# A graph-attention kernel whose first stage no longer writes normalised rows

## The chip, the cores and the metric

The kernel runs on one core of a Trainium2 chip. The metric is device time in microseconds (us), the median of several executions; less is better. The core has TensorE (PE, matrix products), VectorE (DVE), ScalarE (ACT), GpSimd (POOL), SyncE (SP, which here only issues transfers) and 16 DMA engines. PE reads its stationary operand in a separate instruction, LDWEIGHTS, which the profile lists as PEld.

## The reference, cut to what matters

```
x: [10000, 768] f32;  src, dst: 10000 edges sorted by dst, plus one self loop for each node
y  = (x - mean(x)) / sqrt(var(x) + 1e-5)                    # per row
h  = (y @ W1).reshape(N, 4, 512)
e  = leaky_relu(as_n[src] + ad_n[dst], 0.2)                 # as_n = sum_d h * a1_src, ad_n = sum_d h * a1_dst
alpha = softmax of e over the edges that share a dst
h1 = elu(segment_sum(alpha * h[src], dst) + b1)             # [N, 2048]
h2 = a second layer of the same kind with one head, 768 wide
x  = x + h2;   x = x + ffn(layernorm(x))
```

Because as_n = y @ (W1 a1_src), the kernel computes the eight logits of a node as the product of its row with eight vectors v1 [768, 8]. And because y[src] can be summed with its attention weights before the product with W1, layer 1 gathers rows of y, not of h.

## The kernel before

**Stages, one after the other, with a barrier between them.** `stage_normalise` makes normalised rows and logits; `stage_softmax` (sm1) gathers the logits of all edges and writes one record per edge (`rec1`); `stage_layers` does both layers' big products; `stage_softmax` (sm2), `stage_extra_rows` and `stage_output` finish.

**stage_normalise** takes 20 steps of 500 rows (NS = 20), each step four tiles of 125 rows (NT = 4), with four buffers (NB = 4). Before the first step DVE reduces W1 against a1_src and a1_dst to v1 (L349, 48 reductions). In a step DVE normalises in place (L321), takes the statistics of the next step (L289, L293, L295), and with POOL makes the f16 low parts (L327, L271); ACT makes the f16 high parts (L364) and copies transposed tiles out of PSUM (L374); PE transposes a tile (L390), multiplies with v1 as the stationary operand and 125 rows as the moving one (L398), and once a step turns the 8 x 500 logits back (L407), which costs DVE two copies (L316, L310). POOL does one power (L266). SP writes the two parts (`parts`, 1536 f16 values in a row, L238), loads the rows of the step four ahead (L226) and writes the logits (L231).

**stage_layers** works on 20 strips of 500 nodes; a strip is ten windows of 50 nodes (WPS = 10). For a window POOL gathers 128 rows of `parts` (78 edges and 50 own rows) by an indirect DMA into `rows`, which has two buffers (L1117); the gather of window i is issued when PE is done with window i-2. PE multiplies them with the attention weights, `ah` and `al` (L1358 to L1360, 18 products a window). ACT and DVE split the sums into f16 parts `zh` (L1311) and `zl` (L1201). A strip on PE is a first phase of 16 chunks of z @ W1 (L1394 to L1396) and a second phase of 64 steps of g @ W2 (L1418, L1419). The second phase of strip s also holds the windows of strip s+1: window n comes at step 1 + 6n (`AT_STEP`), so window products run between steps of the big product. For strip 0 the ten windows run alone ahead of everything, called the prologue below.

**Slots.** In each strip SP loads the records of the next strip's ten windows (L993, ten transfers) into `slots`, then starts a copy of x (L1076). At chunk 4 DVE computes the row indices from them (`slot_math`, L1165 to L1171); at chunks 5 to 9 it makes two masks each (L1176), which PE uses one chunk later in `look_up` (L1351); at chunk 12 come the weights, at 13 and 14 the first two `spread`. In the second phase DVE does, at window n, `low_parts(n)` (L1201) and `spread(n + 2)` (L1192 to L1196), ACT does `high_parts(n)` (L1311). Each tile of 125 nodes of the result goes through `h2` (L1278, L1280), which has two buffers.

Of the kernel before, what the change touches and what calls it, by code (L numbers as in the profile page):

```python
# [24 lines left out]
ALU = mybir.AluOpType  # L25
# [8 lines left out]
D = 768  # L34
# [17 lines left out]
REC = 12  # L52
# [113 lines left out]
POOL_LOWS = (1, 3)  # L166

def stage_normalise(nc, c, io, dr):

    with ExitStack() as ctx:
        m = Mem(nc, ctx, "nrm")
# [3 lines left out]
        v1 = m.sb("v1", [128, DC, 2 * HEADS])  # L177
        xb = m.sb("xb", [TN, NB, NT, D])
        parts = m.sb("parts", [TN, NB, NT, 2, D], F16)
        stats = m.sb("stats", [TN, NT, 2, 6])  # L180
        mv = m.sb("mv", [TN, NB, NT, 2])
# [3 lines left out]
        logit = m.sb("logit", [TN, NB, NT, 2 * HEADS])  # L185
        pt = [m.ps(f"pt{i}", [128, 2, 512]) for i in range(2)]
        pl = [m.ps(f"pl{i}", [2 * HEADS, NT, 128]) for i in range(2)]
        pb = [m.ps(f"pb{i}", [TN, NT, 2 * HEADS]) for i in range(2)]
        turned_logits = m.sb("turned_logits", [2 * HEADS, 2, NT, 128])
        weights, v_chain, init, held = m.sem("weights"), m.sem("v_chain"), m.sem("init"), m.sem("held")  # L190
        xin, stored, logits_out = ([m.sem(f"{n}{b}") for b in range(NB)] for n in ("xin", "stored", "logits_out"))
        held_pe, w1_in = m.sem("held_pe"), [m.sem(f"w1_in{k}") for k in range(DC)]
        chain, var_ready, pow_ready = m.sem("chain"), m.sem("var_ready"), m.sem("pow_ready")
        xs_ready, hi_ready, lo_ready, pool_lo_ready = (m.sem(n) for n in ("xs_ready", "hi_ready", "lo_ready", "pool_lo_ready"))
        turned, xt_ready, logits_done, row_ready, turned_back, logit_ready = (m.sem(n) for n in (
            "turned", "xt_ready", "logits_done", "row_ready", "turned_back", "logit_ready"))
        block = ctx.enter_context(nc.Block())
        x_rows = io["x"].rearrange("(s p t) d -> s p t d", p=TN, t=NT)
        t_rows = dr.parts.rearrange("(s p t) d -> s p (t d)", p=TN, t=NT)
        l_rows = dr.logit1.rearrange("(s p t) d -> s p (t d)", p=TN, t=NT)  # L200
        VECTOR_LOWS = [t for t in range(NT) if t not in POOL_LOWS]
# [16 lines left out]
        def _(sp):  # L218
# [5 lines left out]
            def load(s, b):  # L224
                for lo, hi in row_parts(TN):
                    sp.dma_start(xb[lo:hi, b], x_rows[s, lo:hi]).then_inc(xin[b], 16)  # L226

            def store_logits(s, b):
                hold(logit_ready, s + 1)
                for lo, hi in row_parts(TN):  # L230
                    sp.dma_start(l_rows[s, lo:hi], logit[lo:hi, b].rearrange("p t k -> p (t k)")).then_inc(logits_out[b], 16)  # L231

            def step(s, b, j):
                hold(hi_ready, NT * s + NT)
                hold(lo_ready, len(VECTOR_LOWS) * (s + 1))
                hold(pool_lo_ready, len(POOL_LOWS) * (s + 1))
                for lo, hi in row_parts(TN):
                    sp.dma_start(t_rows[s, lo:hi], parts[lo:hi, b].rearrange("p t k d -> p (t k d)")).then_inc(stored[b], 16)  # L238
                if within(s + NB):
                    hold(turned, NT * s + NT)  # L240
                    load(s + NB, b)
                if within(s - 2):
                    store_logits(s - 2, (b - 2) % NB)

            load(0, 0)
# [4 lines left out]
            for b in range(1, NB):  # L250
                load(b, b)
            rounds(sp, step)
            store_logits(NS - 2, NB - 2)
            store_logits(NS - 1, NB - 1)
            for b in range(NB):
                sp.wait_ge(stored[b], 32 * NJ)
                sp.wait_ge(logits_out[b], 32 * NJ)

        @block.gpsimd
        def _(pool):  # L260
# [3 lines left out]
            def rough_rstd(u, b):  # L264
                pool.wait_ge(var_ready, u + 1)
                nc.gpsimd.tensor_tensor(rough[:, b], ve[:, b], power[:], ALU.pow).then_inc(pow_ready, 1)  # L266

            def step(s, b, j):
                for t in POOL_LOWS:
                    pool.wait_ge(hi_ready, NT * s + t + 1)  # L270
                    nc.gpsimd.tensor_tensor(parts[:, b, t, 1], xb[:, b, t], parts[:, b, t, 0], ALU.subtract)\  # L271
                        .then_inc(pool_lo_ready, 1)
                if within(s + 1):
                    rough_rstd(s + 1, (b + 1) % NB)
# [5 lines left out]
        def _(dve):  # L280
            PER = 2 * NT + NT + 4

            def statistics(u, b, j):
# [3 lines left out]
                for t in range(NT):  # L287
                    for half in range(2):
                        q.put(nc.vector.bn_stats(stats[:, t, half], xb[:, b, t, half * (D // 2):(half + 1) * (D // 2)]))  # L289
# [7 lines left out]
            def refine(u, b):  # L297
# [6 lines left out]
                q.link(nc.vector.tensor_tensor(rstd[:, b], rough[:, b], sq[:], ALU.mult))  # L304

            def copy_logits(s, b, j):
                dve.wait_ge(turned_back, s + 1)
                if within(s, NB):
                    dve.wait_ge(logits_out[b], 32 * j)
                nc.vector.tensor_copy(logit[:, b], pb[b % 2][:]).then_inc(logit_ready, 1)  # L310

            def copy_rows(s, b):
                dve.wait_ge(logits_done, NT * s + NT)
                if within(s, 2):
                    dve.wait_ge(turned_back, s - 1)
                nc.vector.tensor_scalar(turned_logits[:, b % 2, :, 0:TN], pl[b % 2][:, :, 0:TN], 1.0 / SX, None, ALU.mult)\  # L316
                    .then_inc(row_ready, 1)

            def step(s, b, j):
                for t in range(NT):  # L320
                    nc.vector.tensor_scalar(xb[:, b, t], xb[:, b, t], mv[:, b, t, 0:1], rstd[:, b, t:t + 1], ALU.subtract,  # L321
                                            ALU.mult).then_inc(xs_ready, 1)
                if within(s + 1):
                    statistics(s + 1, (b + 1) % NB, j + (b + 1) // NB)
                for t in VECTOR_LOWS:
                    dve.wait_ge(hi_ready, NT * s + t + 1)
                    nc.vector.tensor_tensor(parts[:, b, t, 1], xb[:, b, t], parts[:, b, t, 0], ALU.subtract).then_inc(lo_ready, 1)  # L327
                if within(s - 1):
                    copy_rows(s - 1, (b - 1) % NB)
                if within(s + 1):  # L330
                    refine(s + 1, (b + 1) % NB)
                if within(s - 2):
                    copy_logits(s - 2, (b - 2) % NB, j - (b < 2))

            nc.vector.memset(xt[:], 0.0).then_inc(init, 1)
            statistics(0, 0, 0)
            refine(0, 0)

            ch = Chain(dve, v_chain)
            dve.wait_ge(weights, 32)  # L340
            for k in range(DC):
                dve.wait_ge(w1_in[k], 16)
                for side, a in ((0, asrc), (1, adst)):
                    for h in range(HEADS):
                        cols = slice(h * HID, h * HID + HID)
                        at = side * HEADS + h
                        if ch.n >= 2:
# [3 lines left out]
                            op0=ALU.mult, op1=ALU.add, accum_out=v1[:, k, at:at + 1]))  # L351
            rounds(dve, step)
            copy_rows(NS - 1, NB - 1)
            copy_logits(NS - 2, NB - 2, NJ - 1)
            copy_logits(NS - 1, NB - 1, NJ - 1)

        @block.scalar
        def _(act):
            def step(s, b, j):
                for t in range(NT):  # L360
                    act.wait_ge(xs_ready, NT * s + t + 1)
                    if t == 0 and within(s, NB):
                        act.wait_ge(stored[b], 32 * j)
# [1641 lines left out]
```

## Time and profile before

| | |
|---|---|
| median of 3 runs | 4167.94 us (4165.6 to 4171.07) |
| profiled execution | 4167.93 us, span 4166.2 us |
| busy | PE 3571.3 us (86%), DVE 2228.8 (53%), ACT 1354.7 (33%), POOL 850.1 (20%) |
| first stage | 0 to about 293 us |
| sm1 | about 293 to 583 us |
| layers | about 583 to 3482 us |
| sm2, extra rows, output | to the end |

The profile gives, for each engine, busy time and the idle time ahead of an instruction with what ended it. PE's granted clock is in tenths or as a share of full speed (1.00 is 2.4 GHz, 0.50 is 1.2 GHz). The profiled execution's span lies 1.7 us below its time, and its time is the median of the runs.

### The profile page before, as it was taken

What the parts mean: (1) busy time and instruction counts of PE and PEld (TensorE: products, weight loads), DVE (VectorE), ACT (ScalarE), POOL (GpSimd) and SP (SyncE); (2) the same over time, 40 slices, a digit from 0 to 9 for tenths busy, and PEclk for the clock granted to TensorE, in tenths of its full rate; (3) what the DMA queues carried; (4) which work ended last, traced back from release to release, by engine and by line L of the source; (5) the groups of instructions that cost most, each with busy time, mean ns of one, the idle gap of its engine ahead of it and who ended that gap; (6) DMA issues with size and microseconds to landing.
All of it is one profiled execution on the core that took longest, in us unless ns stands there. A gap on an engine that the chain in (4) does not pass through costs nothing. (4 is left out here: it accounts for less than half of the span.)

```text
span 4166.2 us, 68773 instructions
## 1 busy us (share of the span) xinstructions
PE 3571.3 (86%) x22440; PEld 2183.9 (52%) x22441; DVE 2228.8 (53%) x5433; ACT 1354.7 (33%) x2327; POOL 850.1 (20%) x1236
## 2 busy tenths in 40 slices
PE   4860019999999999999999999999999996388888
PEld 3640015565556556655655565566556654256565
DVE  8877345334434443443344344434443434699998
ACT  2531104323322332333233223323332333244444
POOL 2448720000000000100000000000000100266665
PEclk9985559999999999999999999999999998699999
DMA  8862011111111111111111111121111100378887
GB/s 256 256 213 83 3 27 41 55 40 46 39 58 36 45 42 54 41 39 48 39 51 38 55 37 43 42 60 36 42 45 40 53 27 15 84 207 231 233 236 209
DMA packets 142471, 337.79 MB, mean 81 GB/s; under 512 B 76839, under 2 KB 76917, under 8 KB 134775
## 3 DMA queue, kind: packets, MB, share of 16 engines
q1 hardware_dynamic: 111976, 240.96, 19.0%
q0 software_dynamic: 29056, 92.87, 8.6%
q8 instruction: 214, 3.51, 0.4%
q14 instruction: 50, 0.41, 0.0%
q10 hardware_dynamic: 1175, 0.05, 0.0%
HBM read 266.01 MB, written 124.25 MB: 94 GB/s over the span
## 5 line engine op out<-in xcount | busy, mean ns | idle before, releaser
L1394 PE MATMUL lay_pm<-lay_zh,w1h 128*128 128x500 f16 x1920 | 718.9, 374 | 26.0 <-DVE lay_h L1280 19.6
L1117 POOL DMA_INDIRECT lay_rows<-parts,lay_idx x200 | 209.7, 1048 | 2536.7 <-PE lay_pz L1360 1616.3
L1395 PE MATMUL lay_pm<-lay_zl,w1h 128*128 128x500 f16 x1920 | 719.2, 375 | 3.2 <-issue 3.1
L1396 PE MATMUL lay_pm<-lay_zh,w1l 128*128 128x500 f16 x1920 | 718.9, 374 | 0.0
L1201 DVE SCALAR_TENSOR_TENSOR lay_zl<-lay_pz,lay_zh 128x400 f16<-128x400 f32 x600 | 319.5, 573 | 708.3 <-ACT lay_zh L1311 708.3
L1311 ACT ACTIVATE lay_zh<-lay_pz 128x400 f16<-128x400 f32 x600 | 297.9, 503 | 1054.2 <-PE lay_pz L1360 1050.2
L1320 ACT ACTIVATE lay_ex<-lay_pm,b1c,scale 128x500 f32<-128x500 f32 x320 | 245.5, 767 | 873.7 <-PE lay_pm L1396 873.7
L1418 PE MATMUL lay_pm<-w2h,lay_gh 128*128 128x512 f16 x1280 | 485.0, 379 | 0.0
L1418 PE MATMUL lay_pm<-w2h,lay_gl 128*128 128x512 f16 x1280 | 483.9, 378 | 0.0
L1418 PE MATMUL lay_pm<-w2l,lay_gh 128*128 128x512 f16 x1280 | 483.4, 378 | 0.0
L1236 DVE TENSOR_SCALAR lay_ex<-lay_ex,scale 128x500 f32<-128x500 f32 x320 | 153.6, 480 | 571.8 <-ACT lay_ex L1320 571.8
L1419 PE MATMUL lay_pm<-w2l,lay_gh 128*128 128x258 f16 x1280 | 349.8, 273 | 0.0
L1419 PE MATMUL lay_pm<-w2h,lay_gl 128*128 128x258 f16 x1280 | 349.8, 273 | 0.0
L1419 PE MATMUL lay_pm<-w2h,lay_gh 128*128 128x258 f16 x1280 | 349.5, 273 | 0.0
L1394 PEld LDWEIGHTS lay_pm<-lay_zh,w1h 128*128 128x128 f16 x1920 | 195.8, 102 | 237.5 <-DVE lay_h L1278 29.1
L1358 PE MATMUL lay_pz<-lay_ah,lay_rows 128*128 128x200 f16 x1200 | 300.5, 250 | 14.3 <-DMA lay_rows<-parts,lay_idx 12.1
L1396 PEld LDWEIGHTS lay_pm<-lay_zh,w1l 128*128 128x128 f16 x1920 | 187.8, 98 | 216.1 <-issue 1.3
L1359 PE MATMUL lay_pz<-lay_al,lay_rows 128*128 128x200 f16 x1200 | 300.4, 250 | 0.0
L1360 PE MATMUL lay_pz<-lay_ah,lay_rows 128*128 128x200 f16 x1200 | 300.3, 250 | 0.0
L1395 PEld LDWEIGHTS lay_pm<-lay_zl,w1h 128*128 128x128 f16 x1920 | 187.7, 98 | 212.8 <-issue 11.0
L1238 DVE SCALAR_TENSOR_TENSOR lay_y<-lay_ex,scale,lay_y 128x500 f32<-128x500 f32 x320 | 236.5, 739 | 79.6 <-ACT lay_y L1322 79.6
L1322 ACT ACTIVATE lay_y<-lay_pm,b1s,scale 128x500 f32<-128x500 f32 x320 | 242.8, 759 | 0.0
(308 smaller groups left out, 5600.6 us busy)
## 6 DMA issues: line engine op xcount, KB each, us to landing
x<-in_x_dram SPq DMA_DIRECT2D x20, 1500.0 KB
out_x<-x SPq DMA_DIRECT2D x100, 288.0 KB
out_own<-h SPq DMA_DIRECT2D x100, 288.0 KB
out_dram<-out_x SPq DMA_DIRECT2D x100, 288.0 KB
nrm_xb<-in_x_dram SPq DMA_DIRECT2D x20, 1344.0 KB
parts<-nrm_parts SPq DMA_DIRECT2D x20, 1344.0 KB
h<-lay_h SPq DMA_DIRECT2D x80, 336.0 KB
nrm_w<-in_L_gnn_W_dram SPq DMA_DIRECT2D x6, 1024.0 KB, 19.6
```

The lines of the kernel that those rows point to most:

```text
L1201: nc.vector.scalar_tensor_tensor(out=window_shape(zl, k, i), in0=pz[k][:, 0:2 * HEADS * WN].rearrange("p (k n) -> p k n", n=WN), scalar=1. ...
L1311: nc.scalar.activation(window_shape(zh, k, i), pz[k][:, 0:2 * HEADS * WN].rearrange("p (k n) -> p k n", n=WN), ACT.Copy, scale=1.0 / SA).t ...
L1320: nc.scalar.activation(ex[:, k % 2], p, ACT.Exp, bias=c.b1[:, k:k + 1], scale=c.scale[:, 8:9])\
L1322: nc.scalar.activation(y[:, k % 2], p, ACT.Identity, bias=c.b1s[:, k:k + 1], scale=c.scale[:, 9:10])\
L1358: pe.matmul(o, high, flat(ah), start=True, stop=False)
L1359: pe.matmul(o, high, flat(al), start=False, stop=False)
L1360: return pe.matmul(o, low, flat(ah), start=False, stop=True)
L1394: pe.matmul(o, c.w1h[:, d, cols], zh[:, d, h], start=(d == 0), stop=False)
L1395: pe.matmul(o, c.w1h[:, d, cols], zl[:, d, h], start=False, stop=False)
L1396: ins = pe.matmul(o, c.w1l[:, d, cols], zh[:, d, h], start=False, stop=(d == DC - 1))
L1418: pe.matmul(oa[:], x[:, k, nodes], wt[:, k, 0:512], **go)
L1419: ins = pe.matmul(ob[:, 0:D + 2 - 512], x[:, k, nodes], wt[:, k, 512:D + 2], **go)
```

## The change

**First stage.** `stage_logits` takes the place of `stage_normalise`. It neither normalises nor writes rows. PE transposes raw rows and multiplies with the transposed rows as the stationary operand and v1 (8 columns) as the moving one, so the result needs no turning back. DVE still takes the statistics, and `finish` makes the logits as (dots - mean * vsum) * rstd / SX. vsum, the column sums of v1, comes once from PE. A row of the table `logit1` is ten values: eight logits, mean, SX * rstd. The first loads are a1_src, a1_dst and W1, then x.

**sm1.** It gathers the ten-value rows; two more copies put mean and scale of both ends of an edge into the record, which has 16 values in place of 12 (also in sm2).

**Layers.** The gathers read raw rows of x (768 f32, as many bytes as before). ACT makes the high part with the row's scale and bias (`high_rows`), DVE normalises in place and subtracts (`low_rows`). In a strip rows 0 and 1 are done at chunks 8 and 10, row n+1 ahead of `high_parts(n)` and `low_parts(n)`. SP issues one more transfer a strip: mean and scale of the 500 own nodes, 8 bytes each. `slot_math` waits for it too and has four more instructions. `h2` has one buffer.

```diff
-                for lo, hi in row_parts(TN):
-                    sp.dma_start(t_rows[s, lo:hi], parts[lo:hi, b].rearrange("p t k d -> p (t k d)")).then_inc(stored[b], 16)
...
+            def finish(s, b, j):
+                q = Chain(dve, table_chain, 2 * s)
+                dve.wait_ge(rstd_ready, s + 1)
...
+                q.put(nc.vector.tensor_tensor(shift[:], mv[:, b, :, 0:1].broadcast_to([TN, NT, 2 * HEADS]),
+                                              vsum[:].rearrange("p (a h) -> p a h", a=1).broadcast_to([TN, NT, 2 * HEADS]),
+                                              ALU.mult))
+                nc.vector.tensor_copy(table[:, b, :, 2 * HEADS], mv[:, b, :, 0])
+                nc.vector.tensor_copy(table[:, b, :, 2 * HEADS + 1], rstd[:, b])
+                q.wait()
+                dve.wait_ge(dots_done, NT * s + NT)
+                q.link(nc.vector.tensor_tensor(shift[:], pd[b % 2][:], shift[:], ALU.subtract))
+                nc.vector.scalar_tensor_tensor(out=table[:, b, :, 0:2 * HEADS], in0=shift[:], scalar=1.0 / SX, ...
...
-                    ins = pe.matmul(pl[b % 2][:, t, 0:TN], v1[:, k], xt[:, t % 2, k, 0:TN], start=(k == 0), stop=(k == DC - 1))
+                    ins = pe.matmul(pd[b % 2][:, t], xt[:, t % 2, k, 0:TN], v1[:, k], start=(k == 0), stop=(k == DC - 1))
...
+            if width > 2 * H:
+                ch.put(nc.vector.tensor_copy(record[:, :, 11:13], gsrc[:, :, 2 * H:2 * H + 2]))
+                ch.put(nc.vector.tensor_copy(record[:, :, 13:15], gdst[:, :, 2 * H:2 * H + 2]))
...
+EARLY_ROWS = {8: 0, 10: 1}
...
+                sp.dma_start(slots[WE:128, :, 11:13],
+                             dr.logit1[bass.ds(SN * q, SN), 2 * HEADS:TW1].rearrange("(i p) w -> p i w", p=WN),
+                             allow_slow_non_contiguous=True).then_inc(slots_in, 16)
...
-                    nc.gpsimd.indirect_dma_start(rows[:, i % 2, :], None, dr.parts[:, :], bass.IndirectOffsetOnAxis(
+                    nc.gpsimd.indirect_dma_start(raw[:, i % 2, :], None, io["x"][:, :], bass.IndirectOffsetOnAxis(
...
+            def low_rows(rc, q, i):
+                at = raw[:, i % 2]
+                dve.wait_ge(hi_done, WPS * q + i + 1)
+                rc.link(nc.vector.tensor_scalar(at, at, mean[:, i:i + 1], scale[:, i:i + 1], ALU.subtract, ALU.mult))
+                nc.vector.tensor_tensor(rows_lo[:, i % 2, 0:D], at, rows_hi[:, i % 2], ALU.subtract).then_inc(lo_done, 1)
...
+            def high_rows(q, i):
+                if i < 2:
+                    act.wait_ge(scale_ready, q + 1)
+                act.wait_ge(gathered[i % 2], 16 * (WPS // 2) * q + 16 * (i // 2 + 1))
+                nc.scalar.activation(rows_hi[:, i % 2], raw[:, i % 2], ACT.Identity, bias=bias[:, i:i + 1],
+                                     scale=scale[:, i:i + 1]).then_inc(hi_done, 1)
...
             def window(q, i, first):
-                pe.wait_ge(gathered[i % 2], 16 * (WPS // 2) * q + 16 * (i // 2 + 1))
+                pe.wait_ge(hi_done, WPS * q + i + 1)
+                pe.wait_ge(lo_done, WPS * q + i + 1)
                 pe.wait_ge(a_ready, WPS * q + i + 1)
```

## Rows read from the trace of the kernel before

**Rows 1.** Busy time by stretch: PE, PEld, DVE, ACT, POOL, then PE clock, DMA share, GB/s.

```profile
0.00:19.40 19.40, 0.00 (x0) 0.01 (x1) 6.38 (x21) 0.00 (x0) 1.99 (x10) 1.00 0.83 268
48.90:60.00 11.10, 9.47 (x48) 7.09 (x48) 10.84 (x25) 6.50 (x8) 4.93 (x3) 1.00 0.06 19
60.00:150.00 90.00, 75.04 (x567) 54.69 (x564) 80.67 (x198) 46.60 (x61) 36.97 (x22) 0.92 0.88 266
643.50:3482.00 2838.50, 2806.03 (x17240) 1647.59 (x17240) 1192.30 (x2659) 901.91 (x1530) 199.66 (x190) 1.00 0.15 44
```

**Rows 2.** Groups of instructions by line, 60 to 290 us: busy us, mean ns, idle before.

```profile
L289 DVE BATCH_NORM_STATS2 nrm_stats<-nrm_xb 125x6 f32<-125x384 f32 x144 | 67.9, 543 | 0.0
L364 ACT ACTIVATE nrm_parts<-nrm_xb 125x768 f16<-125x768 f32 x76 | 63.2, 832 | 69.1 <-DVE nrm_xb L321 69.1
...
L321 DVE TENSOR_SCALAR nrm_xb<-nrm_xb,nrm_mv,nrm_rstd 125x768 f32<-125x768 f32 x76 | 46.4, 673 | 0.8 <-issue 0.7
```

**Rows 3.** Timeline inside one step of the first stage: start, length, engine, line.

```profile
150.13 1.83 DVE L327 TENSOR_TENSOR nrm_parts<-nrm_xb,nrm_parts 125x768 f16<-125x768 f32 x2
...
158.53 0.86 PE L390 MATMUL nrm_pt<-ident,nrm_xb 125*128 125x125 f32 x6
...
159.32 1.45 PE L398 MATMUL nrm_pl<-nrm_xt,nrm_v 128*8 128x125 f32 x12
...
160.70 0.86 PE L390 MATMUL nrm_pt<-ident,nrm_xb 125*128 125x125 f32 x6
...
162.86 0.51 PEld L407 LDWEIGHTS nrm_pb<-ident,nrm_turned_logits 8*125 8x125 f32 x4 [0.21 <-issue]
```

**Rows 4.** Timeline at the first step's start and at the stage's end.

```profile
48.80 2.44 DVE L321 TENSOR_SCALAR nrm_xb<-nrm_xb,nrm_mv,nrm_rstd 125x768 f32<-125x768 f32 x4
...
293.17 0.12 DVE L827 MEMSET sm_dst<- 128x79 int32 x1 [3.51 <-PEq L112]
```

**Rows 5.** Timeline of the prologue of the layers (slot loads, gathers, windows).

```profile
592.36 6.51 ACTq L993 DMA_DIRECT2D lay_slots<-rec  x5
...
599.77 0.17 DVE L1165 TENSOR_TENSOR lay_rel<-lay_slots,lay_woff 128x10 f32<-128x10 f32 x1 [8.36 <-DMA lay_slots<-rec]
...
608.09 0.33 PE L1358 MATMUL lay_pz<-lay_ah,lay_rows 128*128 128x200 f16 x1 [2.03 <-DVE lay_al L1196]
...
626.31 1.00 POOL L1117 DMA_INDIRECT lay_rows<-parts,lay_idx  x1 [3.55 <-PE lay_pz L1360]
...
632.96 1.00 POOL L1117 DMA_INDIRECT lay_rows<-parts,lay_idx  x1 [3.63 <-PE lay_pz L1360]
...
636.81 0.26 PE L1358 MATMUL lay_pz<-lay_ah,lay_rows 128*128 128x200 f16 x1 [2.75 <-DMA lay_rows<-parts,lay_idx]
```

**Rows 6.** Timeline of a strip's first phase: slot_math, first look_up, chunk 9.

```profile
806.42 0.65 SPq L1076 DMA_DIRECT2D x<-in_x_dram  x1
...
809.12 0.16 DVE L1165 TENSOR_TENSOR lay_rel<-lay_slots,lay_woff 128x10 f32<-128x10 f32 x1
...
810.94 0.48 DVE L1236 TENSOR_SCALAR lay_ex<-lay_ex,scale 128x500 f32<-128x500 f32 x1 [0.83 <-ACT lay_ex L1320]
...
812.91 0.47 DVE L1176 TENSOR_SCALAR lay_mask<-lay_pos,lay_rel 128x128 f32<-128x128 f32 x2
...
813.74 0.51 PE L1351 MATMUL lay_look<-lay_slots,lay_mask 128*128 128x5 f32 x4
...
827.21 0.48 DVE L1236 TENSOR_SCALAR lay_ex<-lay_ex,scale 128x500 f32<-128x500 f32 x1 [1.71 <-ACT lay_ex L1320]
```

**Rows 7.** Timeline of a strip's second phase: two gathers, and DVE's low parts.

```profile
860.69 1.00 POOL L1117 DMA_INDIRECT lay_rows<-parts,lay_idx  x1 [6.29 <-PE lay_pz L1360]
...
866.79 1.61 DVE L1201 SCALAR_TENSOR_TENSOR lay_zl<-lay_pz,lay_zh 128x400 f16<-128x400 f32 x3 [5.00 <-ACT lay_zh L1311]
...
868.12 1.00 POOL L1117 DMA_INDIRECT lay_rows<-parts,lay_idx  x1 [6.43 <-PE lay_pz L1360]
```

**Rows 8.** Timeline in sm1: a gather that POOL issues while DVE is busy.

```profile
304.82 2.89 POOL L819 DMA_INDIRECT sm_gsrc<-logit,sm_src  x1 [0.30 <-issue]
```

More of the change, by code:

```diff
@@ L51 @@
 XE = 64
-REC = 12
+REC = 16
 MAX_CHUNKS = E // XE + 1
@@ L351, in _ @@
                             op0=ALU.mult, op1=ALU.add, accum_out=v1[:, k, at:at + 1]))
+            dve.wait_ge(vsum_done, 1)
+            nc.vector.tensor_copy(vsum[:], pv[:]).then_inc(vsum_ready, 1)
+            statistics(0, 0, 0)
+            refine(0, 0)
+            dve.wait_ge(vsum_ready, 1)
             rounds(dve, step)
-            copy_rows(NS - 1, NB - 1)
-            copy_logits(NS - 2, NB - 2, NJ - 1)
-            copy_logits(NS - 1, NB - 1, NJ - 1)
+            finish(NS - 1, NB - 1, NJ - 1)
         @block.scalar
         def _(act):
[L359 to L363, printed above, removed]
-                    nc.scalar.activation(parts[:, b, t, 0], xb[:, b, t], ACT.Copy).then_inc(hi_ready, 1)
-                    if t:
-                        copy_turned(s, t - 1)
-                    elif within(s, 1):
-                        copy_turned(s - 1, NT - 1)
             def copy_turned(s, t):
@@ L421, in _ @@
             pe.wait_ge(v_chain, 2 * HEADS * DC)
+            for k in range(DC):
+                ins = pe.matmul(pv[:], c.ones[:, 0:TN], v1[:, k], start=(k == 0), stop=(k == DC - 1))
+            ins.then_inc(vsum_done, 1)
             rounds(pe, step)
-            logits(NS - 1, NB - 1, NT - 2)
-            logits(NS - 1, NB - 1, NT - 1)
-            turn_back(NS - 2, NB - 2)
-            turn_back(NS - 1, NB - 1)
+            dots(NS - 1, NB - 1, NT - 1)
 class Weights:
@@ L1051, in stage_layers @@
         gathered = [m.sem(f"gathered{b}") for b in range(2)]
-        h2_out = [m.sem(f"h2_out{b}") for b in range(2)]
+        h2_out, scale_ready, hi_done, normed, lo_done, xrows_ready = (m.sem(n) for n in (
+            "h2_out", "scale_ready", "hi_done", "normed", "lo_done", "xrows_ready"))
         b2_in, x_copied = m.sem("b2_in"), m.sem("x_copied")
@@ L1095, in _ @@
             body(NS - 1, False, True)
-            for b in range(2):
-                sp.wait_ge(h2_out[b], 64 * (NT // 2) * NS)
+            sp.wait_ge(h2_out, 64 * NT * NS)
             sp.wait_ge(x_copied, 16 * NS)
@@ L1134, in _ @@
             ch = Chain(dve, setup)
-            nc.vector.memset(rows[:], 0.0).then_inc(init, 1)
+            nc.vector.memset(raw[:], 0.0).then_inc(init, 1)
             nc.vector.memset(gh[:, :, SN:], 0.0).then_inc(init, 1)
@@ L1325, in body @@
                         high(s, k - 1)
+                    if k in EARLY_ROWS and not last:
+                        high_rows(s + 1, EARLY_ROWS[k])
                 high(s, KC - 1)
@@ L1355, in window_products @@
                 o = pz[d // 2][:, d % 2 * HEADS * WN:(d % 2 + 1) * HEADS * WN]
-                high, low = (rows[:, b, part * D + 128 * d:part * D + 128 * d + 128] for part in range(2))
+                high, low = (part[:, b, 128 * d:128 * d + 128] for part in (rows_hi, rows_lo))
                 flat = lambda t: t[:, b].rearrange("p h n -> p (h n)")
```

207 lines of the change are left out of this document (103 added, 104 removed).

## The prediction

> **What bounds the kernel now.** I read the table of busy time by stretch first [rows 1]. In the first stage DMA moves 266 GB/s at a share of 0.88 while DVE is busy 80.67 of 90 us; PE is busy 75 of 90. So two things bind it almost equally, DMA and DVE, and PE comes close behind. In the layers, 643.5 to 3482 us, PE is busy 2806 of 2838.5 us at full clock: there only what keeps PE waiting counts. The groups by line [rows 2] and the timeline of a step [rows 3] then give the pieces of the first stage, the timeline at its ends [rows 4] its length: from 48.80 to 289.66 us (3.51 us ahead of 293.17) for 20 steps, 12.0 us each. The timeline of the prologue [rows 5] shows a latency chain: a gather is issued at 632.96 and PE can start on it at 636.81; gathers of the same buffer parity follow each other at 6.65 us (626.31 to 632.96), and PE idles 2.75 us ahead of the window. Last come two places inside a strip, where slots become indices and masks [rows 6] and where windows are gathered and split [rows 7].
>
> **First stage, the removed bound.** A step reads 1.5 MB and wrote 1.5 MB; now it only reads. At the 266 GB/s of rows 1 that is 5.9 us in place of about 11.8. The tiny table rows (20 kB a step) add nothing. DVE loses four L321 (4 x 0.673 = 2.7 us), two L327 (1.8) [rows 3] and the two logit copies. It keeps eight L289 (8 x 0.543 = 4.3 at most) and some 15 small instructions, and gains `finish` with five small ones; taken at the 0.16 us of a small one [rows 6] these 20 make 3.2 us. So DVE needs some 7 to 7.8 us a step [rows 2]. ACT keeps only L374, a copy of the size of L364 (0.83 us) a tile.
>
> **First stage, the new bound: PE.** A tile now is 2.17 us (158.53 to 160.70), of which the six transposes take 0.79 (158.53 to 159.32) and the product with v1 1.38 for twelve passes [rows 3]. The product is turned round: each of the twelve passes loads 125 columns and moves 8, where it loaded 8 and moved 125. The trace has one near row: the four transposes of L407 load 8x125 and move 8; their loads fill 0.51 us, 0.13 us each at most, and 0.11 if the last one's latency is counted once. Below, look_up (128 columns loaded, 5 moved) puts four passes into 0.51 us including its drain [rows 6], so 0.09 is possible. I take 0.11: 1.33 us for twelve, and 2.12 us a tile. 80 tiles are 170 us, 8.5 us a step. That is above DMA's 5.9 and DVE's 7 to 7.8, so PE binds: it has no wait inside, since it runs two transposed buffers ahead of ACT and four row buffers behind DMA. The bounds are 0.09 (1.87 a tile, 150 us, where DVE would bind at up to 156) and 0.13 (2.35 a tile, 188 us).
>
> The Trainium skill ("TensorE: Matmul & The Clock Gate", LDWEIGHTS (loading the stationary operand)) says that a load takes its number of columns divided by 1.2 in ns, whatever the depth. That is a rule against this change, for 8 columns become 125; by it a pass is 104 ns, a tile 2.04 us, and my sum would be 6 us lower. The 0.51 us for four loads in rows 3 agree with it to within the last load's latency.
>
> **First stage, its start and end.** DVE reached the first step at 48.80 [rows 4], behind 48 reductions of W1 that had to wait for the first MB of it. The first 1.5 MB of x stood ahead of that in the queue; at 268 GB/s [rows 1] that is 5.6 us, and I take 5.3. So PE can start at 43.5. One product for vsum, 1.5 us, puts PE to 45. PE is slow at first: from 48.9 to 60 us its instructions mean 0.197 us busy (9.47/48), later 0.132 (75.04/567) [rows 1], though the table gives the clock as 1.00 there; I add 4 us. Then 45 + 170 + 4 = 219. `finish` adds 0.7, and the last store and the barrier stay as they were: 3.5 us from the last DVE instruction to the first of sm1 [rows 4]. sm1 starts at about 223.3, with some slack for the last store 223.7, **69.5 us earlier**. Bounds: 50 (0.13 a pass) to 80.
>
> **sm1 and sm2.** The 158 gathers stay; their rows have 40 bytes, not 32. What is added: a wider memset, two copies of 128x158 values (0.5 us together, not hidden), and records a third larger, whose store is waited for (162 kB at 266 GB/s, 0.6 us, twice). Together **+1.8 us**.
>
> **Prologue.** The records are in 0.9 us after ACT's issues end (598.87 to 599.77) [rows 5]. SP's new transfer comes right behind its own five, with 500 pieces of 8 bytes; no row shows such a transfer. It can cost nothing (it lands with the others) or 3 us (a whole gather's landing, 3.85, less the 0.9); I take 1. Four more instructions in slot_math, two waits among them: 0.65. The first window then waits also for the second spread (0.7) and for low_rows(0), 0.67 [rows 2] and 0.92 [rows 3] with a wait, 1.7 us. The first window moves from 608.09 to 612.1, +4.1. After that each pair of windows runs through a longer chain: the gather lands; then ACT's high_rows, 0.83 [rows 2] with its semaphore 1.0, then low_rows 1.7, then low_parts of the window before, which DVE has been given behind it and which used to be done by then: 1.6 [rows 7], of which 1.0 was under the gather. 6.65 becomes 6.65 + 1.0 + 1.7 + 0.6 = 9.95, four times: +13.2. Prologue **+17.3 us** (10 to 25).
>
> **Strips.** Per strip DVE gains 10 x 1.7 and ACT 10 x 0.85 us. DVE was busy 1192 of 2838 us and ACT 902 [rows 1], so both have room; the question is who waits. (a) At chunks 8 and 10 low_rows comes behind the masks, and DVE idles 1.71 us ahead of the next chunk there (827.21) [rows 6]: it just fits, and what it is over is hidden by the four PSUM buffers between PE and ACT. (b) In the second phase window n+1's rows need, from the end of window n-1: 1.0 to the issue, 3.85 to land, 1.0 and 1.7, in all 7.6 us. Windows are 7.43 us apart (860.69 to 868.12) and the next but one starts two of these less a window's own 1.6 us later, 13.3: 5.7 us are spare. Queued behind high_rows and low_rows are high_parts(n), low_parts(n) and spread(n+2). Before low_parts DVE idled 5.00 us [rows 7]; low_rows fills 1.7 of it. Nothing reaches PE. (c) One transfer more on SP ahead of the x copy. It issues at 806.42 in place of that copy, 0.65 long, and lands at 808.0 if it needs the same 0.9; slot_math starts at 809.12 [rows 6]. So 1.1 us are left for 500 small pieces. slot_math's four extra instructions (0.65) go into the 0.83 us that DVE idled ahead of 810.94. If the transfer is later, DVE stalls, behind it stand the masks (812.91 to 813.38), and PE wants them for look_up at 813.74: 0.36 + 0.18 us of slack. Each us beyond that costs 19 us in all. Lower bound 0, upper (landing as late as a gather) 1.9 us late, 1.4 x 19 = 26. I take **+4**. (d) One h2 buffer: stores of the tile before were issued 18 us earlier, nothing.
>
> **Sum.** -69.5 + 1.8 + 17.3 + 4 = -46.4: span 4166.2 becomes 4119.8, with the 1.7 us around it 4121.5. The profiled time is the median of the runs, so I predict 4121.
>
> **Rivals.** (1) *Weight loads don't overlap* in the turned-round product: 0.13 a pass, 80 x 0.23 = +18: 4140. For it: L407's row at face value. Against: the reading by latency. Chance 0.12. (2) *The own-node table arrives late* in each strip: +26 less my 4: 4144. For it: 8-byte pieces; against: only 500 of them, spread over many engines. 0.10. (3) *Gathers are held up by DVE.* POOL's issue took 2.89 us with DVE busy beside it [rows 8] against 1.00 [rows 7]; low_rows puts such work beside eight gathers of the prologue: +8 to +15, 4132. In the strips the 5.7 us cover it. 0.06. The Trainium skill ("SBUF — State Buffer", SBUF: two separate sides) calls this the "DVE blocks DMA" trap: while DVE runs in a two-port mode GpSimd can't write descriptors; rows 8 agree in kind. (4) *Slower: rows come too late for the windows of the second phase.* The place is PE's wait for lo_done at each of 190 windows [rows 7]. It begins when the chain of 7.6 us grows past 13.3, and it outweighs the gain from 0.25 us a window (46.4/190); at 0.3 us a window 4178. Against: nothing in rows 7 is near. 0.03. (5) *The change doesn't do what it says*: the first stage stays at 12 us a step for a cause that I don't see, and the 23 us of the other terms are paid: 4190. 0.02. (6) *Better*: 0.09 a pass, DVE binds at 156 us, and the prologue costs 12: 4102. 0.05.
>
> **How the numbers follow.** The forecast has 0.62, its own range 4108 to 4136. Rivals 1 to 3 lie above it and inside 4158; with them and part of 6 the range 4102 to 4158 holds about 0.85 on these numbers. A measurement of this kernel can tell 0.2%, 8.3 us, from no change. Faster 0.93; same 0.02, where rivals 1, 2 and 3 coincide; slower 0.05.
>
> **What would show it.** sm1's first DVE memset at 224 us (213 to 243); in the first stage PE busy near all the time with tiles 2.1 us apart, DMA share near 0.6. Prologue: first window 21 us or so after its stage's first DVE instruction plus 4, same-parity gathers 10 us apart. Strips: 142.6 us apart as before; a wait of PE's look_up for lay_mask would be rival 2, one of the window product for low rows rival 4. I am wrong if PE waits inside the first stage or if the strips get longer by over 1.5 us each.

## The result, and the profile after

The changed kernel takes 4232.95 us (4230.96 to 4235.1, four runs) against 4167.7 us before (4165.6 to 4171.07): ratio 1.0158 (95% interval 1.0143 to 1.0173). I had said 4121, faster at 0.93. It is 65 us slower, 112 us from the forecast and outside its range of 4102 to 4158. The profiled execution has a span of 4232.3 us.

The starts of the stages, read from the two timelines, say where the 66.1 us between the spans arise:

| stretch | before, us | after, us | difference | predicted |
|---|---|---|---|---|
| start to DVE's first instruction of sm1 | 293.17 | 343.03 | +49.9 | -69.5 |
| sm1, to DVE's first of the layers | 290.9 | 290.5 | -0.4 | +0.9 |
| prologue, to the first product of the first phase | 59.4 | 83.3 | +23.9 | +17.3 |
| strips, to DVE's last of the last tile | 2832.9 | 2827.2 | -5.7 | +4 |
| from there to the end | 689.8 | 688.3 | -1.5 | +0.9 |

(My +1.8 for sm1 and sm2 is shared out by halves.) The first stage alone missed by 119 us; the others together are 7 us better than I said, which is partly luck: the prologue is 6.6 worse and the strips 9.7 better. The table of busy time by stretch (columns as in [rows 1]) of the kernel after:

```profile
60.00:150.00 90.00, 90.00 (x443) 90.00 (x444) 35.43 (x150) 19.73 (x25) 7.17 (x7) 1.00 0.44 110
661.40:716.80 55.40, 29.84 (x180) 24.41 (x180) 36.33 (x72) 21.76 (x38) 7.98 (x8) 0.64 0.16 45
671.00:686.00 15.00, 8.21 (x48) 6.79 (x49) 11.43 (x25) 6.73 (x12) 1.99 (x2) 0.50 0.17 48
```

Against [rows 1], in the stretch from 60 to 150 us: DVE fell from 80.67 to 35.43 us in these 90, DMA from 0.88 to 0.44, as wanted; PE is busy all the time, and yet issued only 443 instructions where it had issued 567 in 75 us. The groups by line, 60 to 330 us, show who waits for whom:

```profile
L377 PE MATMUL lgt_pd<-lgt_v,lgt_xt 128*125 128x8 f32 x886 | 186.9, 345 | 0.0
L369 PE MATMUL lgt_pt<-ident,lgt_x 125*128 125x125 f32 x441 | 109.8, 421 | 0.0
...
L308 DVE TENSOR_TENSOR lgt_shift<-lgt_pd,lgt_shift 125x32 f32<-125x32 f32 x19 | 3.6, 192 | 162.5 <-PE lgt_pd L377 162.5
```

PE has no idle time ahead of either group, DVE idles 162.5 us for it. The timeline of two tiles:

```profile
201.17 1.49 PE L369 MATMUL lgt_pt<-ident,lgt_x 125*128 125x125 f32 x6
202.46 2.53 PE L377 MATMUL lgt_pd<-lgt_v,lgt_xt 128*125 128x8 f32 x12
...
204.84 1.49 PE L369 MATMUL lgt_pt<-ident,lgt_x 125*128 125x125 f32 x6
```

A tile takes 3.67 us (201.17 to 204.84), 80 of them 294. The passes take 0.199 us each (2.38/12). But the six transposes have the very shape that they had before, and they take 1.29 us where [rows 3] has 0.79. Something slows all of PE, not only the new product. The kernel before has such stretches too (timeline, then the table by stretch for 49.6 to 59.0, 168.16 to 171.9 and 171.9 to 175.0):

```profile
168.16 1.51 PE L390 MATMUL nrm_pt<-ident,nrm_xb 125*128 125x125 f32 x6 [2.54 <-DVE nrm_xb L321]
169.60 2.38 PE L398 MATMUL nrm_pl<-nrm_xt,nrm_v 128*8 128x125 f32 x12
171.90 0.86 PE L390 MATMUL nrm_pt<-ident,nrm_xb 125*128 125x125 f32 x6
172.70 1.45 PE L398 MATMUL nrm_pl<-nrm_xt,nrm_v 128*8 128x125 f32 x12
```

```profile
49.60:59.00 9.40, 8.47 (x38) 6.28 (x39) 9.25 (x21) 6.46 (x8) 4.93 (x3) 1.00 0.01 1
168.16:171.90 3.74, 3.74 (x18) 2.54 (x18) 3.74 (x8) 2.16 (x3) 1.50 (x1) 0.55 0.99 292
171.90:175.00 3.10, 3.10 (x27) 2.38 (x27) 3.02 (x12) 2.29 (x4) 0.14 (x1) 1.00 0.92 310
```

In the first of the last two stretches, at a granted clock of 0.55 (1.2 GHz for nearly all of it), transposes and product took 1.44 and 2.30 us, in the second, at 1.00 (2.4 GHz), 0.80 and 1.37. But the column says 1.00 also for 49.6 to 59.0, where 38 instructions filled 8.47 us, 0.223 each, against 0.115 at 171.9. And in sm1, where PE has 20 instructions in 290 us, the column says 0.50 before and 1.00 after, with PE busy for the same 6.14 us:

```profile
293.00:580.00 287.00, 6.14 (x20) 2.30 (x20) 157.57 (x255) 23.06 (x10) 198.53 (x159) 0.50 0.18 50
343.03:633.49 290.46, 6.14 (x20) 2.30 (x20) 158.32 (x257) 23.06 (x10) 197.68 (x161) 1.00 0.19 52
```

So the column shows 1.00 from the start of a trace until the first change that is recorded, whatever the engine's pace, and in the kernel after none is recorded before the prologue. Its 1.00 in the first stage is no evidence, while the pace of the transposes is that of 1.2 GHz.

Three theories went into the experiments. A: PE stays at its lower clock through the whole first stage. B: a load of 125 f32 columns costs 0.2 us by itself. C: PE isn't the bound.

### The profile page after: what moved, and what is told of

Read it like the earlier page. It is cut to its first block and busy times, and to the rows that moved or that the text cites. A ratio compares the mean times of both kernels' runs of the same rounds, so it can differ in the third digit from the quotient of the medians.

```text
span 4232.3 us, 69050 instructions
## 1 busy us (share of the span) xinstructions
PE 3670.9 (87%) x22372; PEld 2335.6 (55%) x22373; DVE 2446.1 (58%) x5856; ACT 1491.1 (35%) x2447; POOL 772.9 (18%) x1196
## 3 DMA queue, kind: packets, MB, share of 16 engines
q8 instruction: 119, 1.95, 0.3%
q14 instruction: 135, 1.11, 0.2%
## 5 line engine op out<-in xcount | busy, mean ns | idle before, releaser
L1419 PE MATMUL lay_pm<-lay_zh,w1h 128*128 128x500 f16 x1920 | 718.6, 374 | 26.1 <-DVE lay_h L1285 18.4
L1095 POOL DMA_INDIRECT lay_raw<-in_x_dram,lay_idx x200 | 212.9, 1064 | 2551.6 <-PE lay_pz L1384 1631.0
L1328 ACT ACTIVATE lay_rows_hi<-lay_raw,lay_bias,lay_scale 128x768 f16<-128x768 f32 x200 | 205.1, 1025 | 712.3 <-DMA lay_raw<-in_x_dram,lay_idx 712.3
L1193 DVE SCALAR_TENSOR_TENSOR lay_zl<-lay_pz,lay_zh 128x400 f16<-128x400 f32 x600 | 308.0, 567 | 117.8 <-ACT lay_zh L1320 117.8
L1162 DVE TENSOR_SCALAR lay_raw<-lay_raw,lay_mean,lay_scale 128x768 f32<-128x768 f32 x200 | 135.6, 678 | 381.1 <-ACT lay_rows_hi L1328 380.6
L1382 PE MATMUL lay_pz<-lay_ah,lay_rows_hi 128*128 128x200 f16 x1200 | 305.1, 254 | 26.9 <-DVE lay_zl L1193 22.4
L1383 PE MATMUL lay_pz<-lay_al,lay_rows_hi 128*128 128x200 f16 x1200 | 305.4, 255 | 0.0
L1384 PE MATMUL lay_pz<-lay_ah,lay_raw 128*128 128x200 f16 x1200 | 305.4, 254 | 0.0
```

The lines of the kernel that those rows point to most:

```text
L1095: nc.gpsimd.indirect_dma_start(raw[:, i % 2, :], None, io["x"][:, :], bass.IndirectOffsetOnAxis(ap=idx[:, i:i + 1], axis=0), bounds_check= ...
L1193: nc.vector.scalar_tensor_tensor(out=window_shape(zl, k, i), in0=pz[k][:, 0:2 * HEADS * WN].rearrange("p (k n) -> p k n", n=WN), scalar=1. ...
L1382: pe.matmul(o, high, flat(ah), start=True, stop=False)
L1383: pe.matmul(o, high, flat(al), start=False, stop=False)
L1384: return pe.matmul(o, low, flat(ah), start=False, stop=True)
L1419: pe.matmul(o, c.w1h[:, d, cols], zh[:, d, h], start=(d == 0), stop=False)
```

## The experiments

Times are medians; the kernel before ran beside each group on the same chip: 4162.6 for the first four, 4164.1 for the next four, 4161.9 for the last four.

**1. The product turned back.** v1 stationary again, 125 rows moving, logits turned back on PE.

```diff
-                    ins = pe.matmul(pd[b % 2][:, t], xt[:, t % 2, k, 0:TN], v1[:, k], ...
+                    ins = pe.matmul(pl[b % 2][:, t, 0:TN], v1[:, k], xt[:, t % 2, k, 0:TN], ...
...
+                for t in range(NT):
+                    ins = pe.transpose(pd[b % 2][:, t], turned_logits[:, b % 2, t, 0:TN], c.ident[0:2 * HEADS, 0:2 * HEADS])
```

> The changed kernel with the product of its first stage as in the kernel before: v1 (8 columns) stationary, 125 rows moving, the logits turned back on PE and copied by DVE; all else as changed. Theory A (PE works at its lower clock through the whole first stage of the changed kernel, since products that move 8 columns leave it nearly idle; products that move 125 let it rise as in the kernel before): a tile takes 2.17 us as before plus 0.13 for the turning back, 80 tiles 184 us instead of 293, softmax starts at about 238 instead of 343, total about 4127. Theory B (the clock is not it; a pass that loads 125 f32 columns costs 0.2 us by itself): the same, 4127, since no such pass is left. Theory C (PE is not what is slow, it is the queue or the rows): softmax still starts after 300, total above 4190.

Measured 4142.55, ratio to the kernel before 0.9948 (0.9932 to 0.9965). sm1 (the softmax) starts at 236.5 us (238 expected), transposes are back at 0.79:

```profile
151.59 0.86 PE L383 MATMUL lgt_pt<-ident,lgt_x 125*128 125x125 f32 x6
152.38 0.60 PE L400 MATMUL lgt_pd<-ident,lgt_turned_logits 8*125 8x8 f32 x4
152.91 1.45 PE L391 MATMUL lgt_pl<-lgt_xt,lgt_v 128*8 128x125 f32 x12
154.28 0.86 PE L383 MATMUL lgt_pt<-ident,lgt_x 125*128 125x125 f32 x6
```

C falls; between A and B this run doesn't decide. The total is 15 us above the expected one, and these lie in the strips (2842.0 us in place of 2827.2): see the last group.

**2. A wider moving operand.** The loads stay, PE gets more to do. This kernel is called the wide kernel below.

```diff
-        v1, vsum = m.sb("v1", [128, DC, 2 * HEADS]), ...
+        v1, vsum = m.sb("v1", [128, DC, 128]), ...
...
+            nc.vector.memset(v1[:, :, 2 * HEADS:128], 1.0).then_inc(padded, 1)
```

> The changed kernel with the moving operand of its first stage's product widened from 8 to 128 columns (the other 120 hold ones and their sums are not read); the twelve loads of 125 columns a tile stay. Theory A (lower clock for want of work in the array): more work, yet shorter: six transposes 0.79 us and twelve passes like a transpose, 0.13 each, 2.37 us a tile instead of 3.67, softmax starts at about 244, total about 4133. Theory B (the load costs 0.2 us by itself): not shorter, 3.8 us a tile or more, softmax starts at 355 or later, total 4245 or more.

Measured 4097.31 (one run). With 16 times as many columns moved, the stage is 133 us shorter (softmax at 209.9). Timeline and table of this kernel:

```profile
150.84 1.48 PE L379 MATMUL lgt_pd<-lgt_v,lgt_xt 128*125 128x128 f32 x12
152.15 0.81 PE L371 MATMUL lgt_pt<-ident,lgt_x 125*128 125x125 f32 x6
152.79 1.48 PE L379 MATMUL lgt_pd<-lgt_v,lgt_xt 128*125 128x128 f32 x12
```

```profile
60.00:150.00 90.00, 90.00 (x832) 90.00 (x831) 68.67 (x286) 36.90 (x46) 12.26 (x12) 1.00 0.79 197
```

832 instructions in 90 us in place of 443: a pass takes 0.109 us (1.31/12), the transposes 0.64, a tile 1.95. B falls: the same loads cost half, and the transposes, which nobody touched, cost half too. It was the clock. The clock column bears this out in sm1: it reads 0.50 there in the kernels whose transposes are quick (before, experiment 1 from 240 to 528 us, experiment 2 from 212 to 500) and 1.00 in those whose transposes are slow (after, experiment 3 from 370 to 660, experiment 4 from 350 to 637), so only the quick ones had a change recorded. The total is 36 us under A's 4133, since I had taken a tile at 2.37 us.

**3. One dense product a tile.**

```diff
                 ins.then_inc(dots_done, 1)
+                pe.matmul(pf[:], fill[:, 0:128], fill[:], start=True, stop=True)
```

> The changed kernel with one product added behind each tile's twelve passes: f16, 512 columns, constant operands, its sum never read. Theory A: if this is enough for the clock to rise, a tile takes 0.79 for the transposes, 12 passes of 0.09 to 0.11 and 0.21 for the added product, about 2.2 us, softmax starts at about 230, total about 4119; if it is not enough, theory A gives 3.67 + 0.43 = 4.1 us a tile and 4267. Theory B (loads cost 0.2 us by themselves, transposes 0.21): 3.67 + 0.2 to 0.4, 3.9 to 4.1 us a tile, total 4250 to 4267.

Measured 4291.41, ratio 1.0306 (1.0289 to 1.0324). This much was not enough, a tile takes 4.02 us (152.37 to 156.39), all at the slow pace. Alone it doesn't tell A from B; beside the run before it only says that PE's being busy in the profile's sense (90.00 of 90 us here too) did not raise the clock. The total is 24 us above the highest that either theory gave: the strips, which the edit doesn't touch, took 2859.2 us in place of 2827.2 (see the last group).

```profile
152.37 2.53 PE L380 MATMUL lgt_pd<-lgt_v,lgt_xt 128*125 128x8 f32 x12
154.76 0.59 PE L382 MATMUL lgt_pf<-lgt_fill 128*128 128x512 f16 x1
155.14 1.46 PE L372 MATMUL lgt_pt<-ident,lgt_x 125*128 125x125 f32 x6
156.39 2.53 PE L380 MATMUL lgt_pd<-lgt_v,lgt_xt 128*125 128x8 f32 x12
```

**4. The turned-round product alone, in the kernel before.** The same line exchanged in `stage_normalise`, no turning back.

> The kernel before with one part of the change alone: the product turned round (transposed rows stationary, 8 columns moving), no turning back; rows still normalised and written. Theory A: PE falls to its lower clock here too, a tile takes 3.67 us instead of a share of 12.0 us a step, 14.7 us a step, first stage 53 us longer, total about 4221. Theory B: transposes keep their 0.79 us, passes cost 0.2: 3.2 us a tile, 12.8 a step, total about 4184. Theory C (PE is not what bounds the changed stage): 4168 or less.

Measured 4209.56 (one run), 47 us slower than before by this exchange alone. Tiles 3.67 us apart and transposes at 1.29, as A said; the total is 11 us under A's since the strips took 2821.0 us in place of 2832.9.

```profile
152.22 1.49 PE L376 MATMUL nrm_pt<-ident,nrm_xb 125*128 125x125 f32 x6
153.51 2.53 PE L384 MATMUL nrm_pd<-nrm_v,nrm_xt 128*125 128x8 f32 x12
155.89 1.49 PE L376 MATMUL nrm_pt<-ident,nrm_xb 125*128 125x125 f32 x6
```

**5 to 8: the prologue, and the first stage's start, on the wide kernel.** The rows of the kernel after that the edits start from:

```profile
665.49 1.00 POOL L1095 DMA_INDIRECT lay_raw<-in_x_dram,lay_idx  x1 [11.15 <-PE lay_pz L1384]
...
676.77 1.00 POOL L1095 DMA_INDIRECT lay_raw<-in_x_dram,lay_idx  x1 [7.41 <-PE lay_pz L1384]
```

```profile
670.43 0.68 DVE L1162 TENSOR_SCALAR lay_raw<-lay_raw,lay_mean,lay_scale 128x768 f32<-128x768 f32 x1 [3.83 <-ACT lay_rows_hi L1328]
671.14 0.96 DVE L1163 TENSOR_TENSOR lay_raw<-lay_raw,lay_rows_hi 128x768 f16<-128x768 f32 x1
672.02 1.53 DVE L1193 SCALAR_TENSOR_TENSOR lay_zl<-lay_pz,lay_zh 128x400 f16<-128x400 f32 x3
```

```profile
672.73 0.33 PE L1382 MATMUL lay_pz<-lay_ah,lay_rows_hi 128*128 128x200 f16 x1 [5.25 <-DVE lay_zl L1193]
```

Gathers of one parity are 11.3 us apart (665.49, 676.77, 688.14, 699.47). Of these 11.28 us, 3.88 are the landing, 1.06 high_rows, 1.59 low_rows, 0.71 the first low part queued behind it, and 4.04 the time from window 2's first product (672.73) to the next gather.

*Experiment 5*: for odd windows high_parts and low_parts come ahead of the next window's rows.

```diff
             for i in range(WPS):
+                if i % 2:
+                    low_parts(0, i)
                 if i + 1 < WPS:
                     low_rows(rc, 0, i + 1)
-                low_parts(0, i)
+                if i % 2 == 0:
+                    low_parts(0, i)
```

> The kernel with the 128 columns wide moving operand, and in the prologue of the layers, for odd windows n, high_parts(n) and low_parts(n) come ahead of high_rows(n+1) and low_rows(n+1), on ACT and on DVE. Theory: in the changed kernel the even window's products wait for low parts that stand behind low_rows (672.73 instead of 672.1 for window 2); 0.65 us less for each of four pairs of windows, pairs 10.7 us apart instead of 11.3, total 2.6 us under the wide kernel's 4097, 4094. Rival (the order doesn't matter, the gather's chain alone sets the pairs): 11.3 us, total 4097.

Measured 4090.76 (4088.32 to 4093.41), ratio 0.9828 (0.9812 to 0.9845). From DVE's first instruction to the first phase 78.85 us in place of 81.42: 2.6 less, as expected; in experiments 3, 6 and 7, which keep the order, it is 81.2 to 81.4. The rest of the gain is none of the edit's: the strips took 2821.8 in place of 2825.4, and the first stage ended 1.8 earlier.

*Experiment 6*: PE kept busy between windows.

```diff
                 window(0, i, True)
+                if i % 2:
+                    for n in range(14):
+                        pe.matmul(pm[n % 4][:], c.w1h[:, 0, 0:128], c.w1h[:, 0, 0:512], start=True, stop=True)
```

> The wide kernel with 14 f16 products of 512 columns put behind each odd window of the prologue (operands are weights, the sums are overwritten before they are read). Theory: a part of what the prologue costs over my 17.3 us is PE's lower clock: the profile of the changed kernel gives 0.50 for 671 to 686 us and a window takes 3.0 us at it, 1.5 at full clock. With PE kept busy each pair of windows is 1.4 us shorter and the first 12 products of the first phase 2.5 us, in all 8 us less: 4089. Rival 1 (the added products come before a window that is ready and delay it): 0 to 6 us more, up to 4103. Rival 2 (the clock isn't it): 4097.

Measured 4095.87 (4093.68 to 4097.74). The clock over the prologue's windows (525 to 580 us) rises from 0.63 to 0.79 and gathers of one parity come 9.8 to 10.6 us apart after the first pair, but the prologue takes 81.3 us in place of 81.4. Windows 4, 6 and 8 take 1.71 us in place of 3.16, but window 3 takes 3.16 in place of 1.70, and windows 5, 7 and 9 wait 2.16 us for DVE's low parts where they had waited 0.70; the last one ends at 578.80 us, 578.68 in the wide kernel. (The last 14 products, 3.19 us, fill 3.06 us that PE idles there anyway.) With added products in the way this doesn't say what the lower clock costs by itself.

*Experiment 7*: PE busy ahead of the first stage.

```diff
+            pe.wait_ge(v_chain, 2 * HEADS * DC - 13)
+            for n in range(20):
+                pe.matmul(pf[:], fill[:, 0:128], fill[:], start=True, stop=True)
             pe.wait_ge(v_chain, 2 * HEADS * DC)
```

> The wide kernel with 20 f16 products of 512 columns (constant operands, sum never read) on PE while it waits for the last 13 reductions of W1. Theory: in the wide kernel PE works at its lower clock from 41.9 until about 54.4 us, two tiles and a half; with PE busy before, these 12.5 us become 7 or so: 5 us less, total 4092. Rival (the first step is bound by DVE's statistics and the chain that follows them, so PE's gain is lost): 4097.

Measured 4130.04 (4129.59 to 4140.21): 33 us *slower* than the wide kernel, and neither the theory nor its rival had a place for that. sm1 did start 2.4 us earlier. The strips took 2861.1 us.

*Experiment 8*: eight more gathers issued at once, the rows of windows 2 to 9 in gh and gl.

```diff
                 for i in range(WPS):
+                    if first and i >= 2:
+                        nc.gpsimd.indirect_dma_start(first_raw[i], None, io["x"][:, :], bass.IndirectOffsetOnAxis(
+                            ap=idx[:, i:i + 1], axis=0), bounds_check=N - 1, oob_is_err=False).then_inc(first_in[i - 2], 16)
+                        continue
                     if not (first and i < 2):
                         hold(z_done, 3 * (WPS * q + i - 1))
```

> The wide kernel with the prologue's gathers of windows 2 to 9 issued at once behind the first two, into memory that the first phase uses only later (gh and gl), each with its own semaphore; nothing waits for an earlier window's buffer any more. Theory (the prologue's cost is the chain gather, high_rows, low_rows, window, next gather): without the gather in it DVE sets the pace, 1.65 + 1.53 + 0.86 = 4.0 us a window instead of 5.65, ten windows in 41 us instead of 55, total 14 us under the wide kernel's 4097: 4083. Rival (DVE's work holds up POOL's issues, 2.9 us each as in rows 8 or more, or PE's lower clock sets the pace): at most 5 us less, 4092.

Measured 4079.98 (4078.72 to 4081.22), ratio 0.9801 (0.9785 to 0.9818). The prologue takes 67.4 us, 14.05 less. DVE sets the pace, windows 3.86 us apart on PE, whether they run at the higher clock or, as windows 7 and 8, at 0.50 (timeline):

```profile
535.91 0.25 PE L1406 MATMUL lay_pz<-lay_ah,lay_rows_hi 128*128 128x200 f16 x1 [2.30 <-DVE lay_zl L1210]
539.77 0.25 PE L1406 MATMUL lay_pz<-lay_ah,lay_rows_hi 128*128 128x200 f16 x1 [2.16 <-DVE lay_zl L1210]
```

**9 to 12: what the 20 products did to the strips.** Waits of PE in the strips, and the page's line of PE's instruction queue (packets, MB, share), first of the kernel before, then of experiment 7. A packet is a block of code that is fetched; that q8 is PE's follows from experiments 8 and 9, which differ by PE's products and the memset of their operand: q8 goes from 78 to 214, the other instruction queue from 136 to 135.

```profile
PE lay_pm L1394 <- DVE lay_h L1280: 19.6, 14, 1.7
PE lay_pm L1394 <- DVE lay_h L1278: 3.4, 3, 1.2
q8 instruction: 214, 3.51, 0.4%
```

```profile
PE lay_pm L1429 <- issue: 45.0, 17, 2.9
q8 instruction: 214, 3.51, 0.4%
```

PE idles once a strip, at the turn of its loop (us in total, times, longest): 23.0 us in 17 turns before, 45.0 in experiment 7. DVE, named in the first two lines, isn't what is waited for: its last `lay_h` ends 1.18 us behind PE's last product at every turn, while PE starts again after 1.11 to 1.68 us, at three turns ahead of DVE's end. The table's strips go from the first product of the first phase to DVE's last tile. Experiments 9 to 12 put the products ahead of experiment 8's kernel in four ways.

> The kernel with wide moving operand and all gathers of the prologue issued at once (4080), with the 20 added products ahead of the first stage that made the wide kernel 33 us slower. Theory P (place of code: what that cost came all from PE's turns of the strip loop, 18 idle times of 2.7 us in place of 1.1 to 1.3, since PE's loop code lies 40 instructions later): 2.5 us gained ahead of the layers, the turns 2.7 us again, total 4080 - 2.5 + 30 = about 4108. Rival W (the work that they do, or the memory that they take): also slower here, but then e10 is as slow.

> As the run before, the same 20 products made by a loop of one product: same work at the same place in time, but only a few instructions of code. Theory P: the loop code of the strips keeps nearly its place, the turns stay at 1.1 to 1.3 us, total 4078. Rival W: as slow as e9, 4108.

> As e9 with 10 products instead of 20. Theory P: the turns change with the place of the code; I can't say in which direction at 20 instructions, either 1.1 to 1.3 us (4078) or up to 2.7 (4108). Rival W: half of what e9 adds, 4094.

> As e9 with 40 products instead of 20, begun 12 reductions earlier. Theory P: the turns change with the place of the code, they may be short again; total between 4078 and 4110. Rival W: twice what e9 adds, 4140 or so.

| experiment | us | strips, us | idle of PE at turns | q8 packets |
|---|---|---|---|---|
| 8: none | 4079.98 | 2821.5 | 19.8 in 17 | 78 |
| 9: 20 in line | 4111.15 | 2858.1 | 46.5 in 17 | 214 |
| 10: 20 by a loop of one | 4077.79 | 2824.4 | 20.9 in 17 | 127 |
| 11: 10 in line | 4079.63 | 2820.5 | 18.7 in 17 | 78 |
| 12: 40 in line | 4118.14 | 2863.8 | 45.8 in 17 | 214 |

The idle time makes 27 of the 37 us between 8 and 9, the other 10 are busy time of PE (2810.9 us against 2801.1). In experiment 7, where it is like that, this shows in the products: the group of the first phase has a mean of 377 ns instead of 374, and the granted clock of its strips is 0.99 instead of 1.00. Theory P holds, W falls with experiment 10: the same work costs 33 us or nothing, by how many instructions of code stand ahead of the loop. Experiment 12 came 8 us above the range that I gave P, and 22 below W's 4140.

Experiment 10 (ratio 0.9795, 0.9779 to 0.9811) has the lowest time found, 84 us under the kernel before; 8 and 11 can't be told from it.

## Why the prediction was wrong

**First stage, start: right.** PE's first product came at 42.0 us (43.5 predicted), the first transposes at 44.57 (45).

**First stage, the new bound: the step that failed.** That PE would bind was right, and DVE had more room than I gave it (in experiment 2 it was busy 68.67 of 90 us at 7.82 us a step, so 6.0 a step; I said 7 to 7.8). Wrong were "of which the six transposes take 0.79" and "I take 0.11", taken as prices of the instructions when they are prices at 2.4 GHz; and "PE is slow at first ... I add 4 us", which supposes that the pace doubles after some 10 us as it did before. With 125 or 128 columns moved a pass it doubled (before, experiments 1 and 2), with 8 it did not until the stage's end (after, experiments 3 and 4). 80 x (3.67 - 2.12) is 124 us; less the 4 us that I had added, that is the miss of 119. The row was in front of me: at 49 to 60 us I read 0.197 an instruction at a "clock of 1.00" and didn't ask why. Rival 5, "for a cause that I don't see", at 0.02 and 12 us a step, was the only one near; it took 14.7. Of my two signs of being wrong neither came, PE didn't wait and the strips got shorter; what did show it are the tiles, 3.67 us apart in place of 2.1, and the DMA share, 0.44 in place of near 0.6. At full clock my sum would have been close: 1.95 us a tile (experiment 2) in place of 2.12, since a transpose between such passes takes 0.107, not 0.132. (A step's 1.536 MB at 266 GB/s are 5.8 us, not my 5.9, which changes nothing.)

The Trainium skill ("TensorE: Matmul & The Clock Gate", LDWEIGHTS (loading the stationary operand)) gives, as an estimate worked out from its formula, 104 ns for 125 columns. Experiment 2 agrees at full clock, 109 a pass; the kernel after doesn't at half clock, 199. The same page of the Trainium skill (Part 1: The HAM clock gate) says that the clock follows how busy the array has been and that the ratio is binary. The runs agree with the second (0.50 and 1.00), and with the first only if busy isn't read as the profile's busy time, which was 90.00 of 90 us in the kernel after. That page of the Trainium skill would have given this rival a place.

**sm1 and sm2: not seen.** +1.8 predicted; sm1 came out 0.4 shorter, and what lies behind the layers 1.5. Over the 14 traces sm1 takes 289.6 to 291.5 us and the stretch behind the layers 685.6 to 691.2, so single traces can't show so little.

**Prologue: right in kind, too small.** The first window is 27.97 us behind its stage's first DVE instruction (661.46 - 633.49) against 24.03 before: +3.9 for my +4.1. The pairs take 11.3 in place of 9.95. The part that I undersized is the window itself: 4.04 us from its first product to the next gather, where before 2.8 were left (6.65 - 3.85). That is PE's pace. A window's 18 products took 1.72 us at a granted clock of 1.00 (before, 623.71 to 625.43) and 3.16 at 0.50 (after, 672.73 to 675.89); before, six of the ten windows took 1.72, after, nine took 3.07 to 3.16. I had priced all of them as before. The last window, 3.16 in place of 1.71, adds another 1.4 us behind the last gather. The granted clock averaged 0.64 over the windows (with some 6 us at the start that read 1.00 for want of a record); before, 0.89. Longer gaps ahead of each window and the lower clock come together; that the one causes the other was not shown. That the gather chain is what costs was shown by experiment 8.

**Strips: costs right, a gain missed.** The own-node table issued at 879.18 us and slot_math followed at 882.01 straight behind other DVE work; no wait of look_up, for rows or for the single h2 buffer appears among PE's waits: 0 in place of my +4, and rivals 2 and 4 did not occur. Rival 3 neither: the prologue's gathers took 1.00 us each. Of the 5.7 us less, 3.1 are idle time of PE (26.1 to 23.0 us, of which 3.1 inside the first phase before) and 2.5 its busy time. The turns of the loop idle 23.0 us in both. The kernel before fetched 214 blocks of instructions and the one after 119, so the place of PE's code may be the cause here too, but this pair was not tried by itself: it is not shown.

## What to carry to other kernels

Before turning a product round, ask what it leaves the array to do: an instruction's price read from a trace holds at the clock of that stretch, and a stage in which PE is "busy" all the time with tiny moving operands can sit at 1.2 GHz to its end. Compare the pace of an instruction that the change doesn't touch, here the transposes, which shows the clock where the clock column doesn't. And when a stage that an edit doesn't touch gets longer, look at the loop turns and the instruction queue.

## What the hardware showed that I had not expected

- More work, less time: 128 moved columns in place of 8 made the tile 1.95 us in place of 3.67.
- The clock column reads 1.00 from the start of a trace until the first recorded change, though the pace is that of 0.50 (45 to 343 us of the kernel after, and on through sm1). The mean over that whole kernel, 0.978 against 0.939 before, is too high for the same reason.
- The turn of a long PE loop costs 1.2 us (19.8/17) or 2.7 (46.5/17) by where its code lies; over a kernel that is 43 us (strips of 2820.5 to 2863.8 us with the same work). The slow ones of experiments 8 to 12 fetched 214 blocks of instructions, the quick ones 78 to 127; but the kernels at 214 range from 26 us of idle (before) to 46, so the total doesn't set the size. Two blocks fetched at the turn go with the long idle time, one with the short, without an exception in 238 turns. The Trainium skill ("Runtime: NRT & Kernel Launch", Instruction fetch mechanics) says that a taken branch to code outside the fetched window waits for a fetch. The runs agree as far as the idle time lies at the turn and goes with the fetches there, and show that 20 instructions elsewhere in the kernel can decide how long it is.
